# Output projection of a two-layer FFN by Strassen's seven products, one Trainium2 core

## The reference

```python
x12 = jnp.einsum('bsk,mk->bsm', x, w12) + b12
x1, x2 = jnp.split(x12, 2, axis=-1)
x4 = jax.nn.silu(x1) * x2
return jnp.einsum('bsm,nm->bsn', x4, w3) + b3
```

## Time and profile before

| what | us |
|---|---|
| median of 3 runs | 906.12 |
| lowest and highest run | 897.71 and 1540.92 |
| span of the profiled execution | 911.4 |
| TensorE busy in it | 859.9 |
| gate steps, about | 382 to 727.5 |
| output projection, first matmul to the end of the span | 727.6 to 911.4 |

### The profile page before, as it was taken

One profiled execution on the slowest core, in us unless ns is written; L12 is line 12 of the kernel. 1 busy time (PEld: TensorE's weight loads), 2 busy tenths in 40 slices (PEclk: granted clock), 3 DMA queues, 4 the chain that ended last, 5 costly groups with the idle time before them and its releaser, 6 DMA issues.

```text
span 911.4 us, 10875 instructions
## 1 busy us (share of the span) xinstructions
PE 859.9 (94%) x4175; PEld 726.6 (80%) x4175; DVE 322.7 (35%) x365; ACT 140.1 (15%) x178; POOL 137.7 (15%) x74
## 2 busy tenths in 40 slices
PE   5877899999999787999999999999999989999998
PEld 4855788888888787888888888888888868888886
DVE  3484652453331744430303122121213842222221
ACT  3541010110100322310111012110101210001100
POOL 2341332323221000000000000000000312222221
PEclk9597899999999978999999999999999999999999
DMA  8733631322319999502020202020204644444441
GB/s 227 235 111 121 179 116 48 115 85 77 123 39 171 140 101 95 72 24 69 24 70 25 80 24 69 23 69 23 69 23 147 194 131 139 138 138 138 138 149 58
DMA packets 70891, 91.51 MB, mean 100 GB/s; under 512 B 6648, under 2 KB 54184, under 8 KB 70864
## 3 DMA queue, kind: packets, MB, share of 16 engines
q1 hardware_dynamic: 69792, 90.30, 38.9%
q10 hardware_dynamic: 896, 0.60, 0.2%
q0 software_dynamic: 176, 0.24, 0.1%
HBM read 63.58 MB, written 27.54 MB: 100 GB/s over the span
## 4 chain that ended last, share of the span: by engine, by line
PE 83%; DMA 7%; DVE 5%; SPq 2%; issue 1%; ACT 1%; POOL 0%; ACTq 0%; DVEq 0%; POOLq 0%
PE ps L1076 83%; DMA x<-x_scratch 3%; DVE w_t L938 1%; DVE wk_lo L799 1%; DMA raw<-in_L_ffn_w 1%; SPq L424 1%; SPq L341 1%; DMA raw<-in_L_ffn_kernel 1%; DMA biask_s<-in_L_cond_bias_k 1%; DMA lora_b_scratch<-lb_c_lo 1%; ACT wk_hi L637 1%; DVE z L868 1%; DVE lb_t L899 1%; DMA lb<-lora_b_scratch 0%; SPq L401 0%
## 5 line engine op out<-in xcount | busy, mean ns | idle before, releaser
L1076 PE MATMUL ps<-c_hi,w_hi 128*128 128x512 f32 x512 | 199.3, 389 | 0.0
L1076 PE MATMUL ps<-c_hi,w_lo 128*128 128x512 f32 x512 | 199.2, 389 | 0.0
L1076 PE MATMUL ps<-c_lo,w_hi 128*128 128x512 f32 x512 | 199.2, 389 | 0.0
L593 POOL TENSOR_TENSOR res<-x_in,b_s 128x1024 f32<-128x1024 f32 x16 | 50.6, 3172 | 559.6 <-DMA b_s<-in_L_ffn_b 435.2
L1076 PEld LDWEIGHTS ps<-c_hi,w_hi 128*128 128x128 f32 x512 | 96.1, 188 | 20.0
L1076 PEld LDWEIGHTS ps<-c_lo,w_hi 128*128 128x128 f32 x512 | 96.1, 188 | 19.9
L1000 DVE SCALAR_TENSOR_TENSOR h_s<-ps,b_s,silu_s 128x512 f32<-128x512 f32 x32 | 24.0, 750 | 248.5 <-PE ps L1076 248.5
L1076 PEld LDWEIGHTS ps<-c_hi,w_lo 128*128 128x128 f32 x512 | 96.1, 188 | 19.8
L1076 PE MATMUL ps<-w_hi,h_hi 128*128 128x512 f32 x256 | 100.2, 391 | 4.3 <-DVE w_lo L959 4.3
L1076 PE MATMUL ps<-w_lo,h_hi 128*128 128x512 f32 x256 | 100.3, 392 | 0.0
L1076 PE MATMUL ps<-w_hi,h_lo 128*128 128x512 f32 x256 | 100.3, 392 | 0.0
(11 more groups left out here) (121 smaller groups left out, 784.7 us busy)
## 6 DMA issues: line engine op xcount, KB each, us to landing
raw<-in_L_ffn_w SPq DMA_DIRECT2D x96, 128.0 KB, 3.4
x_in<-in_x SPq DMA_DIRECT2D x16, 512.0 KB, 4.4
x_scratch<-x_t SPq DMA_DIRECT2D x16, 512.0 KB, 3.0
x<-x_scratch SPq DMA_DIRECT2D x64, 128.0 KB, 6.9
h_scratch<-h_s SPq DMA_DIRECT2D x32, 256.0 KB, 2.4
h_in<-h_scratch SPq DMA_DIRECT2D x16, 512.0 KB, 4.5
x_in<-x_scratch SPq DMA_DIRECT2D x16, 512.0 KB, 5.2
out<-res SPq DMA_DIRECT2D x15, 512.0 KB, 3.2
```

Of the source, the lines that this page charges most:

```text
L593: pool.tensor_tensor(res[s][:, :].rearrange("p (b q) -> p q b", q=PH), x1_in[s][:, :].rearrange("p (q b) -> p q b", q=PH), b3_s[:, :].rear ...
L1076: return pe.matmul(o, l, r, start=start, stop=stop)
```

## The change

The 2048 x 1024 h and the 1024 x 1024 w3 are taken in 2 x 2 blocks: a unit is two tiles (a11, a12 / a21, a22, each 128 rows by 512 of the inner index), w3 is B11, B12, B21, B22 (512 x 512 each). Seven products of 12 matmuls (4 inner blocks x 3) replace eight. w3 gets the sums T1 to T4, h gets s1 to s4 for each unit, each split into high and low. One bank, x (0 or 1 by the unit), accumulates four products in turn (P0, P2, P4, P6) and VectorE reads it after each of them; y is bank 2, w bank 3. There are seven adds per unit into the two res tiles. Loads of h come for two tiles at once (1 MB). In the last gate step, all of w3 is turned first (blocks 0 to 3 before `hidden(7, 0)`, 4 to 7 before `hidden(7, 1)`), GpSimd makes T3, and SP's order is new.

SyncE (SP), from the last gate step on:

```diff
-            load_w3(0)
-            load_w3(1)
+            for c in range(6):
+                load_w3(c)
             store_h(NJ - 1, 0)
-            load_w3(2)
-            load_w3(3)
-            sp.wait_ge(g2_mm, 4 * NJ + 1)
-            sp.wait_ge(h_stored[0], 16 * NJ)
-            for t in range(2):
-                load_h(t, t)
-                load_x1(t, t)
-            store_h(NJ - 1, 1)
-            load_w3(4)
-            load_w3(5)
-            sp.wait_ge(g2_mm, 4 * NJ + 2)
-            sp.dma_start(b3_s[:, :], b3.partition_broadcast(P)).then_inc(b3_in, 16)
-            store_h(NJ - 1, 2)
             load_w3(6)
             load_w3(7)
+            store_h(NJ - 1, 1)
+            store_h(NJ - 1, 2)
+            sp.wait_ge(g2_mm, 4 * NJ + 3)
+            sp.wait_ge(h_stored[0], 16 * NJ)
+            load_h(0, 0)
+            sp.wait_ge(h_stored[1], 16 * NJ)
+            load_x1(0, 0)
+            sp.wait_ge(h_stored[2], 16 * NJ)
+            sp.dma_start(b3_s[:, :], b3.partition_broadcast(P)).then_inc(b3_in, 16)
             store_h(NJ - 1, 3)
...
+            load_x1(0, 1)
+            sp.wait_ge(g2_mm, 4 * NJ + 4)
+            load_h(1, 1)
+            sp.wait_ge(h_stored[3], 16 * NJ)
...
+            def rows_of_out(u, s, load_x1_only=False):
+                for a in range(2):
+                    sp.wait_ge(res_made, u * 2 + 1 + a)
+                    load_x1(u + 1, a)
+                for a in range(2):
+                    store_tile(u, s, a, u * 7 + 13 + a)
+                if not load_x1_only:
+                    sp.wait_ge(o_mm, u * 7 + 7)
+                    load_h(u + 2, s)
```

GpSimd and ScalarE:

```diff
+            pool.wait_ge(turned, W12_USES + 8)
+            pool.wait_ge(g2_mm, 4 * NJ + 2)
+            pool.tensor_tensor(T3[0], B22[0], B12, ALU.subtract).then_inc(t3_made, 1)
+
             pool.wait_ge(b3_in, 16)
-
-            def residual(s, loaded, free):
-                pool.wait_ge(x1_loaded[s], loaded)
+            pool.wait_ge(g2_mm, 4 * NJ + 4)
...
+            act.wait_ge(turned, W12_USES + 4)
+            w3_hi_part(B11)
+            w3_hi_part(B21)
             silu(7, 0)
-            w3_hi_part(0)
-            w3_hi_part(1)
+            act.wait_ge(turned, W12_USES + 8)
+            w3_hi_part(B22)
+            act.wait_ge(w3_sum_made, 1)
+            w3_hi_part(T1)
             silu(7, 1)
-            w3_hi_part(2)
-            w3_hi_part(3)
...
+            act.wait_ge(w3_sum_made, 2)
+            w3_hi_part(T2)
+            silu(7, 2)
+            act.wait_ge(t3_made, 1)
+            w3_hi_part(T3)
...
             h_hi_part(0, 0, 16)
-            silu(7, 2)
+            silu(7, 3)
+            act.wait_ge(w3_sum_made, 3)
+            w3_hi_part(T4)
+            hs_hi_part(0, 0)
```

VectorE:

```diff
+            def h_sums(u, s):
+                a11, a12 = h_f[s][:, 0:QH, 0, :], h_f[s][:, QH:, 0, :]
+                a21, a22 = h_f[s][:, 0:QH, 1, :], h_f[s][:, QH:, 1, :]
+                s1, s2, s3, s4 = [hs_f[s][:, n] for n in range(4)]
+                dve.tensor_tensor(s1, a21, a22, ALU.add).then_inc(hs_made, 1)
+                dve.tensor_tensor(s3, a11, a21, ALU.subtract).then_inc(hs_made, 1)
+                dve.wait_ge(hs_made, u * 4 + 1)
+                dve.tensor_tensor(s2, s1, a11, ALU.subtract).then_inc(hs_made, 1)
+                dve.wait_ge(hs_made, u * 4 + 3)
+                dve.tensor_tensor(s4, a12, s2, ALU.subtract).then_inc(hs_made, 1)
...
+            ADDS = ((0, 0, 0), (3, 0, 0), (0, 0, 1), (2, 1, 1), (0, 1, 1), (2, 0, 1), (0, 1, 0))
+            PARTIAL = {1: 0, 4: 3, 5: 2}
+
+            def add(u, s, n):
+                b, a, half = ADDS[n]
+                if n == 0:
+                    dve.wait_ge(res_made, u * 2 + 2)
+                if n in PARTIAL:
+                    dve.wait_ge(out_made, u * 7 + 8 + PARTIAL[n])
+                dve.wait_ge(o_mm, u * 7 + n + 1)
+                cols = res[s][a][:, half * HALF:(half + 1) * HALF]
+                dve.tensor_tensor(cols, bank(b if b else s), cols, ALU.add).then_inc(out_made, 1)
+
+            for c in range(4):
+                turn_w3(c)
             hidden(7, 0)
-            turn_w3(0)
-            turn_w3(1)
-            w3_lo_part(0)
-            w3_lo_part(1)
+            for c in range(4, 8):
+                turn_w3(c)
+            w3_sum(T1, (B12,), B11[0], 1)
+            w3_lo_part(B11, 1)
             hidden(7, 1)
...
+            w3_sum(T2, B22, T1[0], 2)
+            w3_lo_part(T1, 4)
             hidden(7, 2)
...
+            w3_sum(T4, B21, T2[0], 3)
+            w3_lo_part(B21, 4)
+            w3_lo_part(T2, 5)
+            dve.wait_ge(h_loaded[0], 16)
+            h_sums(0, 0)
+            h_lo_tile0(0, 0)
             hidden(7, 3)
...
+            def out_unit(u, s, loaded):
+                for n in range(3):
+                    add(u, s, n)
+                dve.wait_ge(h_loaded[1 - s], loaded)
+                h_sums(u + 1, 1 - s)
+                add(u, s, 3)
+                h_lo_tile0(u + 1, 1 - s)
+                add(u, s, 4)
+                h_lo_tile1(u + 1, 1 - s)
+                add(u, s, 5)
+                h_lo_sums(u + 1, 1 - s)
+                add(u, s, 6)
```

TensorE (`out_product` is 12 matmuls; products P0 to P6 in this order):

```diff
+                pe.wait_ge(h_lo_made, u * 3 + 1)
...
+                out_product(x, a11, B11, True)
...
+                    pe.wait_ge(out_made, u * 7 + 2)
+                out_product(w, a12, B21, True)
+                pe.wait_ge(h_lo_made, u * 3 + 3)
...
+                pe.wait_ge(out_made, u * 7 + 8)
+                out_product(x, s2, T2, False)
+                out_product(y, s1, T1, True)
...
+                pe.wait_ge(out_made, u * 7 + 10)
+                out_product(x, s3, T3, False)
...
+                pe.wait_ge(out_made, u * 7 + 11)
+                out_product(y, s4, B22, False)
...
+                pe.wait_ge(out_made, u * 7 + 12)
+                out_product(x, a22, T4, False)
```

More of the change, by code:

```diff
@@ L145, in layered_kernel @@
         silu_s = [at(f"silu_s{s}", [P, HALF], 144.25 + 2 * s) for s in range(2)]
[L146 to L155, removed]
+        h_s = [at(f"h_s{s}", [P, HALF], k) for s, k in enumerate((148.25, 150.25, 160.25, 164.25))]
+        QH = KT // 2
+        UNITS = TILES // 2
+        w3_n1 = at("w3_n1", [P, NJ, HALF], 166.25)
+        w3_n2 = at("w3_n2", [P, NJ, HALF], 0)
@@ new lines, in w3_slot @@
+        def w3_slot(name, lo_kb, hi_kb, whole=None):
+            return (at(f"{name}_f", [P, QH, HALF], lo_kb)[:, :, :] if whole is None else whole, at(f"{name}_hi", [P, QH, HALF], hi_kb, F32R),
+                    at(f"{name}_lo", [P, QH, HALF], lo_kb, F32R))
+        B11 = w3_slot("w3_b11", 166.25, 182.25, w3_n1[:, 0:QH, :])
+        B21 = w3_slot("w3_b21", 174.25, 190.25, w3_n1[:, QH:, :])
+        B12 = w3_n2[:, 0:QH, :]
+        B22 = w3_slot("w3_b22", 8, 152.25, w3_n2[:, QH:, :])
+        T1 = w3_slot("w3_t1", 64, 72)
@@ new lines, in layered_kernel @@
+        T2 = w3_slot("w3_t2", 16, 24)
+        T3 = w3_slot("w3_t3", 80, 88)
+        T4 = w3_slot("w3_t4", 32, 40)
+        h_f = [at(f"h_f{s}", [P, NJ, 2, P], 96 + 16 * s) for s in range(2)]
+        h_lo = [at(f"h_lo{s}", [P, NJ, 2, P], 96 + 16 * s, F32R) for s in range(2)]
+        hs_f = [at(f"hs_f{s}", [P, 4, QH, P], 104 + 16 * s) for s in range(2)]
+        hs_lo = [at(f"hs_lo{s}", [P, 4, QH, P], 104 + 16 * s, F32R) for s in range(2)]
+        h_hi0 = [at(f"h_hi0{s}", [P, NJ, P], (199.75, 128)[s], F32R) for s in range(2)]
@@ L495, in _ @@
-            with sp.Fori(1, TILES // 2) as i:
-                for s in range(2):
[L497 to L504, removed]
@@ new lines, in _ @@
+            dve.wait_ge(h_loaded[1], 16)
+            h_sums(1, 1)
+            add(0, 0, 3)
+            h_lo_tile0(1, 1)
+            add(0, 0, 4)
+            h_lo_tile1(1, 1)
+            add(0, 0, 5)
+            h_lo_sums(1, 1)
+            add(0, 0, 6)
+            def out_unit(u, s, loaded):
[10 more added lines that the diff above has]
+                add(u, s, 6)
@@ L1068, in _ @@
+            with dve.Fori(0, UNITS // 2 - 1) as i:
+                out_unit(i * 2 + 1, 1, i * 16 + 32)
+                out_unit(i * 2 + 2, 0, i * 16 + 32)
+            for n in range(7):
+                add(UNITS - 1, 1, n)
         @block.tensor
@@ L1291, in _, with out_product @@
                     gate_step(i * 2 + k, k)
-            def out_tile(t, s, first=False):
-                pe.wait_ge(h_lo_made, t + 1)
-                pe.wait_ge(out_made, t * 2 + 2)
-                for half in range(2):
-                    if first:
-                        pe.wait_ge(w_lo_made, W12_USES + 4 * (half + 1))
-                    for j in range(NJ):
-                        last = products([bank(2 * s + half)], h_hi[s][:, j, :], h_lo[s][:, j, :],
-                                        [w3_hi[half][:, j, :]], [w3_lo[half][:, j, :]], j == 0, j == NJ - 1)
-                    last.then_inc(o_mm, 1)
+            def out_product(o, left, right, first):
+                for k in range(QH):
```

(5 more changed lines are left out.)

177 lines of the change are left out of this document (107 added, 70 removed).

## The result

The changed kernel takes 949.4 us (median of 4 runs, 942.9 to 953.9) where the kernel before takes 905.4 beside it: a ratio of 1.048, with a 95% interval of 1.043 to 1.053. (One of the four runs of the kernel before, at 1540.9 us, is far off and is left out of the ratio.) Slower, by about 44 us; the forecast was 953. The profiled execution has a span of 952.1 us, where the working gave 958.9.

The account below looks back on a forecast made before the run. TensorE, busy 94% of the span, was taken as the bound. Start 752.1 + unit 0 29.6 + units 1 to 6 154.8 + unit 7 19.0 + 3.4 gave a span of 958.9; less 5.3, 953 us, range 908 to 967.

Parts of the forecast that it names:

- start of P0: First product of the output projection, after the gate: starts at 752.1 us, leaving TensorE 24.5 us idle instead of 4.5.
- P0 to P5 of unit 1: Output projection: 29.6 us for the first unit, then 13.6 to the sixth product of the next, which starts 5.1 late.
- the five units to P5 of unit 6: Steady units of the output projection: 25.8 us each, made of 19.0 products, 5.1 stall and 1.7 slower clock.
- signs of being wrong: Prediction fails if gaps within the units are under 1 us, or the first product starts before 740.
- What is removed: Output projection on TensorE: 768 matmuls become 672, so 96 fewer at 0.2267 us, -21.8 us.
- The price of the lock: VectorE and GpSimd exclude each other on two SBUF tiles; residuals delay P5 by 5.1 us in units 1 to 6.
- rival B: Collisions come, but stalls near 3.5 us stay short of the gap that drops the clock: 933 us, chance 0.27.
- Before the first product: Last gate step: added w3 turns, splits, sums and h load put h at 744.4 and the first product at 752.1.
- Unit 0: First unit of the output projection: 19.04 us of products plus 1.7 clock and 8.9 waits, 29.6 us in all.
- Rival C: Residuals miss VectorE's work in steady units, only the start is late: 913 us, or 899 without front collisions; chance 0.15.
- Rival E: Chain of w3 loads and transposes before the first product is longer still: +8 to +15 us, 965; chance 0.04.
- Rival D: Only the lower product count shows, start as well hidden as before and all units full: 884 us, chance 0.04.

Follow-up runs that it names:

- with the wait: Changed kernel, with GpSimd's residuals also waiting until VectorE has made the second low part of that unit's h: 906.4 us, ratio 0.999.

## Why the prediction was right

**The sum.** Point by point, forecast and profile:

| step | forecast | measured |
|---|---|---|
| start of P0 | 752.1 | 746.5 |
| P0 to P5 of unit 1 | 48.3 | 47.5 |
| the five units to P5 of unit 6 | 129.0 | 127.3 |
| from there to the end of the span | 29.5 | 30.8 |
| span | 958.9 | 952.1 |

The forecasts of the middle rows are the text's own terms: 29.6 + 13.6 + 5.1, and 5 x 25.8. Of the 6.8 us of difference 5.6 lie in the start. The time is off by less than the span, 3.6 us, and that is luck: the 5.3 us taken off the span for the median were 2.7 here.

**The signs.** None of the signs of being wrong came. The gap at the gate's end, said to be 20 to 26 us and to wait for h_lo, was 19.4 and stands under "issue"; the four sums, said to be 9 us long, were 8.2; the gaps at P5, said to be 4 to 5, were 4.1.

**What is removed** was right: 96 matmuls, 21.8 us, and the run without residual instructions shows them gained but for the start.

**The price of the lock** was right in kind and place. Two residuals fall into the four sums in each of the six units, one VectorE instruction standing for each. The Trainium skill, page "SBUF — State Buffer", section "Who interferes with whom", says the same of a VectorE instruction with two SBUF inputs against a GpSimd one that reads SBUF; the 0.68 us sums at 3.57 and 3.38 agree, and so do the transposes (4.43 beside GpSimd, 4.38 without) and the adds from PSUM (0.68 or 0.69) that pay nothing. I took 5.1 at P5; 4.1 is the idle time shown. Add 2 was done at 9.0 us of its unit, near the 8.9 taken, but the two residuals held the sums up for 5.6 (3.57 + 3.38 less twice 0.68) and not 6.2, and the sums follow each other a little closer than their lengths (785.13 to 785.73 for one of 0.68). The clock came as said: 1.7 each was taken, and it was some 1.6 behind the gaps of units 1, 3 and 5 and 2.8 behind those of units 2, 4 and 6, where 13 or 14 matmuls in place of 8 ran slow. So 5.1 + 1.7 = 6.8 per unit measured 25.47 - 19.04 = 6.4, and rival B, which had the stalls stop short of the clock's fall, did not come. Its premise failed too: it put the point at which the clock falls between gaps of 3.0 and 4.1 us, and in unit 0 the clock fell behind 2.07.

**Before the first product** three terms were mis-sized, and one step was wrong. T3 was put at 6.2 us, twice a residual, and took 4.61; the Trainium skill's 4.5, which stood beside it as the other sum, was the nearer. The residual was a bad unit: its output is reordered by columns, and it takes 2.9 for 1024, where the plain form takes 1.29 for 512 columns and 4.61 for 2048. The turns ended at 717.2, not 720.3. The load of h landed by 739.9, not 744.4. The wrong step is "Only then can SP pass store_h(7, 2), and load_h(0, 0) ... is queued behind it", as the thing that sets the start. VectorE's list ended at 739.69 and h landed 0.2 later, by coincidence; with the load 5.8 us ahead of need, P0 stood idle about as long as before (19.3 us). The prediction's own figures said so: its list of VectorE ends at 745.0, behind its load at 744.4, and 752.1 is summed from the 745.0. So the start came out near for the list's sake, not for the queue's. The lists of T2, T4 and the low parts, which I let run "meanwhile", were themselves the bound. The first residual did slip in as said, but onto h_lo_tile0 (3.83) and not between the sums and it.

**Unit 0.** +2.8, +3.0, +3.1 were given for P2, P4, P5; the idle times shown are 2.1, 0.4 and 2.5, but the clock fell there two more times, which I had not counted. The two errors, 3.9 too much idle and some 3.2 of clock left out, nearly cancel, by luck.

**Rival C**, the residuals out of the way, is what the experiments built. It was priced at 899 to 913 and gave 899.5 without the residual instruction, 906.4 with the wait, 900.6 and 902.7 with the residual on VectorE. Its 24.6 us for unit 0 has no working; from P0 to unit 1 it was 22.5 without the residual instruction. **Rival E**, a longer chain of w3, did not come: the turns ended 3.1 us earlier than taken. **Rival D**, 884, would need the start hidden as well; the shortest stretch reached is 175.3, where D needs 162.3. Whether the rest can be hidden (the turns of w3 begun in an earlier gate step) was not tried.
